# Splitting the experts' weights straight into SBUF, most of them during the expert stage

## The reference

```python
x = L0_attn_x
xn = _layernorm(x, axis=-1)
x = x + _L0_attn_ref(xn, Wq, bq, Wk, bk, Wv, bv, Wo, bo, projection) + _L0_ffn_ref(xn, router_w, w1, w2)

# attention, per head: Qp, Kp = relu(normalised Q, K @ projection) + 0.1
# KV = Kp^T V;  out = Qp KV / (Qp . sum Kp);  then @ Wo + bo

# experts: 8 experts, 2 per token, at most 2049 tokens each
logits = xf @ router_w.T                  # the two best, weights renormalised
h = silu(einsum('ech,ehf->ecf', buf, w1)) # w1: 8 x 256 x 1024
out_buf = einsum('ecf,efh->ech', h, w2)   # w2: 8 x 1024 x 256
combined = sum over the token's two experts of weight * out_buf
```

## Time and profile before

| | us |
|---|---|
| median of 3 runs | 1385.09 (1381.79 to 1393.39) |
| the profiled execution | 1387.81 |
| its span in the trace | 1386.2 |
| of it, attention stage up to the first expert matmul | 623.6 |
| expert stage, first matmul to the end of the span | 762.6 |

### The profile page before, as it was taken

One profiled execution on the slowest core, in us unless ns is written; L12 is line 12 of the kernel. 1 busy time (PEld: TensorE's weight loads), 2 busy tenths in 40 slices (PEclk: granted clock), 3 DMA queues, 4 the chain that ended last, 5 costly groups with the idle time before them and its releaser, 6 DMA issues.

```text
span 1386.2 us, 38134 instructions
## 1 busy us (share of the span) xinstructions
PE 1202.6 (87%) x14334; PEld 976.1 (70%) x14334; DVE 839.0 (61%) x1942; ACT 627.9 (45%) x1108; POOL 715.1 (52%) x660
## 2 busy tenths in 40 slices
PE   4678787878787878439899999999999999999997
PEld 2545464646454546228788888888888888888886
DVE  6789988999998886834344344344344444434432
ACT  4567776777776767323232332333233233233222
POOL 3327272727272727442555555555555555555553
PEclk9889987999998978569999999999999999999998
DMA  4105050606050406079644444444444444444451
GB/s 148 47 33 184 32 184 32 185 32 184 33 184 32 154 32 215 2 226 284 187 78 78 74 72 79 76 69 79 76 73 77 76 77 75 73 74 76 78 73 16
DMA packets 156139, 133.73 MB, mean 96 GB/s; under 512 B 93825, under 2 KB 144258, under 8 KB 154946
## 3 DMA queue, kind: packets, MB, share of 16 engines
q1 hardware_dynamic: 122338, 95.58, 24.2%
q0 software_dynamic: 33632, 35.71, 16.3%
HBM read 61.83 MB, written 52.61 MB: 83 GB/s over the span
## 4 chain that ended last, share of the span: by engine, by line
PE 70%; DVE 18%; issue 5%; ACT 4%; DMA 1%; POOL 1%; SPq 0%; DVEq 0%; ACTq 0%; POOLq 0%
PE bank L953 27%; PE bank L969 26%; DVE area L1342 4%; PE bank L777 3%; PE bank L805 3%; PE bank L836 3%; DVE area L1244 2%; PE bank L822 2%; PE bank L862 2%; PE bank L741 1%; PE bank L716 1%; DVE area L1367 1%; DVE area L1374 1%; DVE area L1236 1%; DVE area L1333 1%
## 5 line engine op out<-in xcount | busy, mean ns | idle before, releaser
L953 PE MATMUL bank<-area 128*128 128x256 f16 x3408 | 388.6, 275 | 21.0 <-DMA area<-xg 17.1
L1488 DVE TENSOR_SCALAR area<-area 128x512 f16<-128x512 f32 x284 | 128.5, 452 | 425.1 <-ACT area L642 421.8
L969 PE MATMUL bank<-area 128*128 x3408 | 383.5, 273 | 0.0
L953 PEld LDWEIGHTS bank<-area 128*128 x3408 | 335.6, 99 | 62.8 <-issue 21.8
L969 PEld LDWEIGHTS bank<-area 128*128 128x128 f16 x3408 | 333.3, 98 | 38.7
L1146 POOL DMA_INDIRECT out_dram<-area,mt x142 | 228.8, 1611 | 236.2 <-ACT area L652 209.7
L1062 POOL DMA_INDIRECT slot_table<-area x128 | 147.4, 1151 | 215.3 <-DVE dump_f L1321 174.4
L642 ACT ACTIVATE area<-bank 128x512 f32<-128x512 f32 x284 | 169.5, 597 | 191.7 <-PE bank L953 191.2
L652 ACT ACTIVATE area<-bank,mt 128x256 f32<-128x256 f32 x142 | 59.5, 470 | 329.5 <-PE bank L969 329.5
L1490 DVE SCALAR_TENSOR_TENSOR area<-area 128x512 f16<-128x512 f32 x284 | 196.7, 693 | 9.8
L1139 POOL DMA_INDIRECT xg<-xn_split,mt x142 | 143.0, 1007 | 45.8 <-issue 42.7
(11 more groups left out here) (177 smaller groups left out, 1371.6 us busy)
## 6 DMA issues: line engine op xcount, KB each, us to landing
area<-in_w_dram SPq DMA_DIRECT2D x32, 512.0 KB, 6.0
experts_split<-area SPq DMA_DIRECT2D x32, 512.0 KB, 4.1
area<-experts_split SPq DMA_DIRECT2D x8, 2048.0 KB, 8.0
area<-in_x_dram SPq DMA_DIRECT2D x16, 512.0 KB, 7.1
xn_split<-area SPq DMA_DIRECT2D x16, 512.0 KB, 2.9
out_dram<-area SPq DMA_DIRECT2D x32, 256.0 KB, 5.1
xg<-xn_split,mt POOLq DMA_INDIRECT x142, 2.9
area<-xg SPq DMA_TRANSPOSE x142
```

The source lines that it names most:

```text
L953: mm = nc.tensor.matmul(big[j][:, i2 * TS:(i2 + 1) * TS], we[:, bass.ds(e * EXPERT + (k * 2048 + wl * 1024 + c * P), P)], moe_xT[t % XT][: ...
L969: mm = nc.tensor.matmul(yb[:, a * D:(a + 1) * D], hT[u % 2][:, c, hl, a * P:(a + 1) * P], we[:, bass.ds(e * EXPERT + off, D)], start=(c == ...
L1488: v.tensor_scalar(hT[u % 2][:, 2 * j:2 * j + 2, 0, :], h32[j], H_SCALE, None, ALU.mult).then_inc(mh_step, 1)
```

## The change

Each chunk is now split straight into its place in `we`; `w_st`, `w_store`, `experts_split` and the eight reloads are gone, and `w_raw` becomes two tiles outside the overlaid area. Expert 0's four chunks are split in the turns b = 0 to 3, one in each. The 28 chunks of experts 1 to 7 are split in the expert stage, chunk t with tile t: ACT's part after the tile's silu, DVE's after its `hidden_split`. SP loads chunk t + 2 behind the row turn of tile t, once chunk t has been split. The waits on the two stores of xn replace those on the stores of the halves.

```diff
         def w_load(sp, e, c):
...
-            if c >= 2:
+            if e > 0 or c >= 2:
                 hold(sp, w_lo, e * 4 + c - 1)
             sp.dma_start(dst, src).then_inc(w_in[c % 2], 16)
-
-        def w_store(sp, e, c):
-            dst = ws_rows[bass.ds(e * P, P), c, :]
-            hold(sp, w_lo, e * 4 + c + 1)
-            sp.dma_start(dst, w_st[c % 2].rearrange("p h n -> p (h n)")).then_inc(w_out[c % 2], 16)
...
         (sp_turn)
-            w_store(sp, b, 0)
-            w_load(sp, b, 2)
-            w_store(sp, b, 1)
-            w_load(sp, b, 3)
             out_store(sp, b, 0)
             out_store(sp, b, 1)
-            w_store(sp, b, 2)
-            if body:
-                w_load(sp, b + 1, 0)
-            w_store(sp, b, 3)
-            if body:
-                w_load(sp, b + 1, 1)
             out_store(sp, b, 2)
             out_store(sp, b, 3)
+            if b < 4:
+                w_load(sp, (b + 2) // 4, (b + 2) % 4)
...
         (sync engine, after the body turns)
-            for e in range(E):
-                if e == 1:
-                    sp_turn(sp, B - 1, "tail")
...
-                    for n in range(2):
-                        sp.wait_ge(out_stored[n], 16 * 2 * B)
-                    sp.wait_ge(meta_stored, 16 * TOPK * NT * B)
-                    sp.wait_ge(tab_ready, 1)
-                if e > 0:
-                    sp.wait_ge(experts_in, 16 * e)
-                sp.dma_start(we[:, e * EXPERT:(e + 1) * EXPERT],
-                             wsplit[e].rearrange("p c h n -> p (c h n)")).then_inc(experts_in, 16)
-                if e > 0:
-                    rows_turn(sp, e - 1)
-            sp.wait_ge(experts_in, 16 * E)
-            for t in range(E - 1, MT):
+            sp_turn(sp, B - 1, "tail")
+            for t in range(MT):
                 rows_turn(sp, t)
+                if t + 2 < 4 * (E - 1):
+                    w_load(sp, (t + 2) // 4 + 1, (t + 2) % 4)
...
-            nc.scalar.activation(w_st[c % 2][:, 0, :], w_raw[c % 2], ACT.Copy, scale=R_SCALE).then_inc(w_hi, 1)
+            nc.scalar.activation(we_parts[:, e, c, 0, :], w_raw[c % 2][:, :], ACT.Copy, scale=R_SCALE).then_inc(w_hi, 1)
...
         (act_turn: w_high(act, b, 0..3) go; behind the second v_copy of the half:)
+            if b < 4:
+                w_high(act, 0, b)
...
         (act, expert stage)
                     silu(act, g * GRP + u, u, first and u == 0)
+                    if g * GRP + u < 4 * (E - 1):
+                        w_high(act, (g * GRP + u) // 4 + 1, u % 4)
...
         (hidden)
-            hold(pe, experts_in, e * 16 + 16)
+            hold(pe, w_lo, e * 4 + 4)
...
         (dve_turn: w_low(dve, b, 0..3) go; behind the last out_drain:)
+            if b < 4:
+                w_low(dve, 0, b)
...
         (dve, expert stage)
                     hidden_split(dve, t, u)
+                    if t < 4 * (E - 1):
+                        w_low(dve, t // 4 + 1, t % 4)
```

More of the change, by code:

```diff
@@ L173, in moe_attention @@
         xg = sb("xg", [P, XR, 2, 2 * D], F16)
-        AREA = 16384 + 166528 + 3072
+        AREA = 169600
         EXPERT = 4 * 2 * 1024
         area = sb("area", [P, AREA // 4], F32)
+        w_raw = [sb(f"w_raw{i}", [P, 1024], F32) for i in range(2)]
         cursor = [EXPERT // 2]
@@ L227, in moe_attention @@
         bo_hl = osb[0][0:1, 1, :].bitcast(F16).rearrange("p (h n) -> p h n", h=2)
-        w_raw = [view([1024], F32) for _ in range(2)]
-        w_st = [view([2, 1024], F16) for _ in range(2)]
         bn = view([NT, 6], F32)
@@ L322, in moe_attention @@
         w_hi, w_lo = sem("w_hi"), sem("w_lo")
-        w_out = [sem(f"w_out{i}") for i in range(2)]
         dve_prep, dve_attn, dve_table = sem("dve_prep"), sem("dve_attn"), sem("dve_table")
         tab_ready = sem("tab_ready")
-        experts_in = sem("experts_in")
         meta_in = sem("meta_in")
@@ L370, in moe_attention @@
         w2_rows = w2.rearrange("e f d -> (e f) d")
-        ws_rows = wsplit.rearrange("e p c h n -> (e p) c (h n)")
+        we_parts = we.rearrange("p (e c h n) -> p e c h n", e=E, c=4, h=2)
         def w_load(sp, e, c):
@@ L376, in w_load @@
                 src = w1_rows[bass.ds(e * D + c * P, P), :]
-                dst = w_raw[c % 2]
+                dst = w_raw[c % 2][:, :]
             else:
@@ L474, in _, with w_high @@
             sp_turn(sp, B - 2, "body", x_next=False)
-            for n in range(2):
-                sp.wait_ge(w_out[n], 16 * 2 * (E - 1))
-            for e in range(E):
-                if e == 1:
-                    sp_turn(sp, B - 1, "tail")
[L482 to L485, removed]
-                        sp.wait_ge(out_stored[n], 16 * 2 * B)
-                    sp.wait_ge(meta_stored, 16 * TOPK * NT * B)
-                    sp.wait_ge(tab_ready, 1)
-                if e > 0:
-                    sp.wait_ge(experts_in, 16 * e)
-                sp.dma_start(we[:, e * EXPERT:(e + 1) * EXPERT],
-                             wsplit[e].rearrange("p c h n -> p (c h n)")).then_inc(experts_in, 16)
-                if e > 0:
-                    rows_turn(sp, e - 1)
-            sp.wait_ge(experts_in, 16 * E)
-            for t in range(E - 1, MT):
+            sp_turn(sp, B - 1, "tail")
+            for t in range(MT):
                 rows_turn(sp, t)
-        def w_high(act, e, c, first=False):
+                if t + 2 < 4 * (E - 1):
+                    w_load(sp, (t + 2) // 4 + 1, (t + 2) % 4)
+        def w_high(act, e, c):
             hold(act, w_in[c % 2], (e * 2 + c // 2 + 1) * 16)
-            if not (first and c < 2):
-                hold(act, w_out[c % 2], (e * 2 + c // 2) * 16)
-            nc.scalar.activation(w_st[c % 2][:, 0, :], w_raw[c % 2], ACT.Copy, scale=R_SCALE).then_inc(w_hi, 1)
+            nc.scalar.activation(we_parts[:, e, c, 0, :], w_raw[c % 2][:, :], ACT.Copy, scale=R_SCALE).then_inc(w_hi, 1)
         def qk_read_half(act, b, half, n0=0, n1=4):
@@ L579, in oT_copy, with act_turn @@
                 nc.scalar.copy(oT[:, 2 * j:2 * j + 2], src).then_inc(attn_taken, 1)
-        def act_turn(act, b, phase, first=False):
+        def act_turn(act, b, phase):
             body = phase == "body"
@@ L603, in act_turn @@
                 xT_copy(act, phase, b + 1, 1)
-            w_high(act, b, 0, first)
-            w_high(act, b, 1, first)
             if body:
@@ L620, in act_turn @@
                 qk_read_half(act, b + 1, 1, 0, 4)
-                w_high(act, b, 2)
                 squares_copy(act, phase, b + 1, 1)
@@ L624, in act_turn @@
             if not body:
-                w_high(act, b, 2)
-                w_high(act, b, 3)
                 return
@@ L679, in _ @@
             k_relu(act, 0, 1)
-            act_turn(act, 0, "body", first=True)
+            act_turn(act, 0, "body")
             for b in range(1, B - 1):
@@ L687, in _ @@
                 act.wait_ge(out_stored[n], 16 * 2 * B)
-                act.wait_ge(w_out[n], 16 * 2 * E)
+                act.wait_ge(xs_stored[n], 16 * B)
             def group(g, first=False, last=False):
@@ L1419, in dve_turn @@
                 qk_halves(dve, b + 1, 0, 2, 4)
-            w_low(dve, b, 0)
-            w_low(dve, b, 1)
             if body:
@@ L1432, in dve_turn @@
                 norms(dve, phase, b + 1, 1)
-            w_low(dve, b, 2)
             out_drain(dve, phase, b, 1, first)
-            w_low(dve, b, 3)
+            if b < 4:
+                w_low(dve, 0, b)
             if body:
```

5 lines of the change are left out of this document (2 added, 3 removed).

## The result

| | before | after |
|---|---|---|
| median | 1385.28 us (1381.79 to 1393.39, 4 runs) | 1451.12 us (1447.94 to 1453.08, 4 runs) |
| ratio | | 1.0464 (95%: 1.0414 to 1.0515) |
| profiled execution / its span | 1387.81 / 1386.2 | 1453.08 / 1451.5 |
| first expert matmul | 623.6 | 602.7 |
| end of the last expert matmul | 1377.0 | 1442.2 |

The kernel became slower by 66 us, as forecast in sign and place, but by less than half of the 153 us forecast, and 4 us outside the range. The trace splits it: up to the first expert matmul 20.9 us were saved, and the expert stage grew by 86.2 us.

A forecast was written before the change was run, and what follows sets the result against it. PE was taken to bound the expert stage, a ring of DVE and POOL attention. 1387.8 + 170 (stalls and clock) + 11.8 - 6.5 - 9.6 - 13 = 1540.5, against the runs' median 1538 us; range 1455 to 1605.

The forecast's parts named there:

- What w_load waits for, and what is queued behind it: Expert stage, SP's queue: load waits for chunk t's low half, row turn of tile t + 1 behind it, near +3.75 us.
- Rival D: Expert stage: row turns still in time, PE never waits, only the savings count, 1356 us; chance 0.04.
- The stall: Expert stage, before each of tiles 2 to 26: PE waits 4.5 us for the row turn, bounds 2.0 and 7.4.
- rival C: Expert stage: transposes wait for the whole load, stall 7.4 us, clock 2.8, in all 1626 us; chance 0.08.
- The clock: Expert stage: PE's granted clock drops after each stall, costing 2.3 us each, between 1.5 and 2.8.
- Rival B: Expert stage: short stall of 2 us and no drop of the clock, 1413 us in all; chance 0.12.
- my own case: Rival A, the forecast itself: expert-stage stalls with clock drops, its own range 1465 to 1600 us; chance 0.74.
- Tile 1: Expert stage: no expert_out ahead, so the full 9.7 us wait plus 2.3 of clock, less 0.2: +11.8 us.
- Tile 6 of the kernel before: Expert stage: its 3.75 us wait and 2.77 us slow restart go away, -6.5 us.
- The change of stage: Attention to experts: first row turn no longer behind a 2 MB load, needs only its gather; -9.6 us, bounds -6 and -12.
- Attention: Turns 0 to 6: POOL's scatters and refining no longer slowed beside w_low, 1.6 to 2.2 us a turn, -13 us.
- The sign that I named for it: Attention windows: turns shorter by about 2 us, DVE's wait for POOL longer, 4 us or more.

The follow-up runs named there:

- e1_ahead: Changed kernel with SP turning the rows three tiles ahead, in front of the load; 1426.96 us, ratio to the kernel before 0.9765; on another chip 1358.46, 0.9783.
- e5: Changed kernel with two more operations like w_low, results unused, on DVE ahead of each w_low of the expert stage; ratio to the kernel before 1.1235.
- e3_no_load: Changed kernel without the loads of chunks 2 to 27 in the expert stage, SP's wait on w_lo kept; 1502.75 us, ratio to the kernel before 1.0278.
- e4: Changed kernel with one more operation like w_low, result unused, on DVE ahead of each w_low of the expert stage; ratio to the kernel before 1.0937.
- e8: Changed kernel with four w_raw tiles, so the load needn't wait for the newest chunk's low half; two runs, ratios to the kernel before 1.0277 and 1.0308.
- e6: e1_ahead with unused two-input DVE operations put back where w_low stood in attention turns 0 to 6; 1440.20 us, on another chip 1367.07.
- e7: e1_ahead with unused one-input DVE operations (batch-norm statistics) put back at w_low's places in attention turns 0 to 6; 1428.99 us.

## Why the prediction was right or wrong

It was right in sign and place and in what makes PE wait, and wrong in the two terms per tile: the length of the stall, and a drop of the clock at each of them.

- **What w_load waits for, and what is queued behind it**: right. The load's issue was put at +3.3 us and the transposes' at +3.75; the trace has +3.23 and +3.68. The waits are where they were forecast, 26 of them, none after tile 26, and e1_ahead shows that the order makes the whole loss of the expert stage. Rival D had no ground.
- **The stall: the step that failed.** "So hidden(t + 1) starts near +3.75 + 5.57 = +9.3 ... I add 0.4: +9.7." It starts at +8.0. I took the wait from the one row where PE stood waiting for a row turn, tile 6, "because tile 6 is the same pair of DMAs with a waiting PE". It was not the same case: POOL's adds were being issued beside its transposes, which they are not in the changed kernel, where they come 2.9 us later. e5 moved the transposes back beside the adds and measured 5.8 instead of 4.4. The stall was 2.74 us on average, not 4.5: 25 x 1.8 = 44 us too much. What fits it instead is the load ahead: +3.23 for its issue, 3.6 to its landing, 1.24 more to the matmul make +8.1, a stall of 2.8. That is rival C's mechanism, which I had priced at 5.1 to 7.4 with landings measured in attention (6.0 to 8.3). With nothing ahead on the queue, in e3_no_load, it is 3.95 us from issue to matmul, of which 2.50 are the issue of both, and waits from 1.7 us up. The Trainium skill's fixed cost of about 2 us ("DMA: Bandwidth & Descriptors", the anatomy of one DMA), which I had set aside, gave an estimate of 1.8 us of stall; that section is on DMAs that GpSimd issues, and these are SP's, but e3's 1.7 is near it.
- **The clock**: the second half of the miss, and it follows largely from the first. "I expect a drop each time": 18 of the 25 hidden behind a stall ran without one, which the prediction had itself named as a sign of being wrong. I took 2.3 us for each wait; 14.4 / 25 = 0.58 was measured. For the 4.5 us that I had forecast the 2.3 would have been about right: e4 with 3.8 us of wait has 2.6, e5 with 6.2 has 2.3. Over the traces of the changed kernel, its repeat, e3, e4, e5 and both e8 (tiles 2 to 26) no hidden was slow (over 6 us) behind a wait under 2.0 us (0 of 41), 36 of 81 were between 2.0 and 3.5 us, and 52 of 53 above. The changed kernel's waits lie in the middle, so a term taken as linear in the number of waits was the wrong form. In that middle it isn't the length alone: 17 of 24 were slow between 2.0 and 2.5 us, but 8 of 40 between 2.5 and 2.75. What else decides stays open. The loop that the Trainium skill describes ("TensorE: Matmul & The Clock Gate", on oscillation in real kernels), with a slow restart in each step, is e4 and e5 (49 of 50 hidden slow), not the changed kernel (7 of 25).
- **The two together**: 25 x 6.8 = 170 forecast, 68.5 + 14.4 = 82.9 measured. That is 87 us, all of the miss. Rival B (short stall, clock up, 1413) was off by 38 us and the forecast by 87: the truth lay between them, in the 52 us between B's 1413 and the 1465 at which my own case began, and there no case stood.
- **Tile 1**: +11.8 forecast; 8.14 of wait and 7.95 instead of 5.24, less the 0.17 before: +10.7.
- **Tile 6 of the kernel before**: -6.5, right for the profiled execution, but the second trace of the same kernel has no wait there and 2.0 us in two others. It was a chance of one execution, and the stall was taken from it.
- **The change of stage**: -9.6 forecast, from 57.2 to 47.9 us, -9.3.
- **Attention**: -13 forecast. From placing turn 0 to placing turn 7 468.9 us became 455.9, -13.1; before that 1.5 were lost, so -11.6. That the sum came so near is in part luck: it was forecast as 1.6 to 2.2 in every turn, but 5.1 of it lie in the one step from turn 6 to 7, and in the repeated traces 466.8 became 457.2, -9.6, of which 5.4 lie there. The reason, POOL slowed beside w_low, is borne out by e6 against e7 and by POOL's own times. The sign that I named for it was wrong: DVE's wait for POOL was to grow to 4 us or more a turn and fell to 0.6 or 1.2 in most. POOL's scatters now end before DVE's guess of the norms, so in six turns POOL waits for DVE, by 0.7 us.

The sum of what was measured: 82.9 + 10.7 - 6.5 - 9.3 - 11.6 = 66.2, and -0.7 for a first hidden that was less slow (7.02 against 7.69): 65.5, against 65.3 between the two spans.

## What to carry to other kernels

A load that waits for a consumer must not stand in an engine's list ahead of a DMA that the next step needs, since the engine issues the list in order; put what is needed soonest in front, here three tiles ahead, and the same change gains 2% instead of losing 5%. When the length of a new wait is taken from a single old one, check in the timeline what else was in flight there, and in a second trace whether it comes back, above all when the result hangs on it 25 times. And where a wait can be short or long enough to lose the clock, give the middle its own case in the range.

## What was not expected of the hardware

- Slow clock behind waits: none behind 41 waits under 2.0 us, 36 behind 81 between 2.0 and 3.5, and 52 behind 53 above, so in e4 1.1 us more of wait (2.74 to 3.84) cost 3.1 us per tile, (918.2 - 839.6) / 25, with hidden from 5.8 to 7.8 us in the mean.
- A pair of DMA transposes, 2.5 us of issue, was usable after 3.95 us alone, 4.4 behind a 512 KB load (1.24 us after that load's landing in the median, early or late), and 5.8 with POOL's adds into DRAM issued beside them as well.
- 24 DVE operations of 1.2 us with two SBUF inputs, three or four in a turn, cost 13.2 us (8.6 on another chip) and lengthened POOL's scatters from 1.08 to 1.16 us in the mean; 39.6 us of DVE work with one input and hardly any output cost 2.0 and lengthened nothing.
- The same kernel took 1461 us on one chip and 1386 on the others. In e1_ahead, traced on both kinds, the difference is in the attention stage, where DVE (up to 7.6 us at a time) and ACT (up to 15.0) stood waiting for something that the profile calls only "remote". The expert stage did not differ: 746 to 747 us.
